# Grouped attention layers: values' last two quarters joined in the next tile, denominators joined with its first quarter, reciprocals on 16 columns

## What is computed

```
xn   = x * rsqrt(mean(x*x) + eps) * w
q    = xn @ wq                    # 16 heads of 32
k, v = context @ wk, context @ wv # 4 heads of 32, each shared by 4 heads of q
out  = softmax(q k^T / sqrt(32)) v
x    = x + out @ wo
```

## Time and profile before

| | |
|---|---|
| median of 3 runs | 4080.01 us (4079.27 to 4080.47) |
| the profiled execution | 4083.46 us |
| its span, first to last instruction | 4081.7 us |
| granted TensorE clock, mean | 0.989 of full |
| TensorE busy | 3991.6 us, 98% |
| VectorE, ScalarE, GpSimd busy | 2434.2, 2094.2, 2035.3 us |

### The profile page before, as it was taken

How to read it: one execution, slowest core, us unless ns; L and a number is a source line. 1 busy time by engine, 2 the same in 40 slices (tenths; PEclk the granted TensorE clock), 3 DMA queues, 4 the chain that set the end, 5 groups by cost and what they waited for, 6 DMA issues and landing times. The chain is left out here.

```text
span 4081.7 us, 52317 instructions
## 1 busy us (share of the span) xinstructions
PE 3991.6 (98%) x19446; PEld 2636.9 (65%) x19446; DVE 2434.2 (60%) x3455; ACT 2094.2 (51%) x2728; POOL 2035.3 (50%) x1097
## 2 busy tenths in 40 slices
PE   9999999998999999999968999999999999999999
PEld 7888888886566666666544555555555555555555
DVE  3221210011755566556638888888888888888885
ACT  3111221121544454444527776776677677767765
POOL 0000000001655566556736777677667677776766
PEclk9999999998999999999979999999999999999999
DMA  5343522233645555555423333333333333333332
GB/s 185 129 135 133 170 96 85 79 114 91 161 125 139 136 135 134 137 135 132 116 70 88 88 89 88 100 101 100 84 100 91 90 99 98 99 89 92 100 78 67
DMA packets 312792, 447.01 MB, mean 110 GB/s; under 512 B 44728, under 2 KB 116408, under 8 KB 312552
## 3 DMA queue, kind: packets, MB, share of 16 engines
q1 hardware_dynamic: 312552, 443.84, 38.8%
HBM read 215.07 MB, written 102.77 MB: 78 GB/s over the span
## 5 line engine op out<-in xcount | busy, mean ns | idle before, releaser
L1943 DVE TENSOR_REDUCE a_max_cols<-a_ps 128x1 f32<-128x512 f32 x1536 | 1028.5, 675 | 265.5 <-PE a_ps L2077 257.2
L1826 ACT ACTIVATE a_probs<-a_ps 128x1024 f32<-128x1024 f32 x768 | 774.6, 1024 | 378.3 <-PE a_ps L2108 372.7
L2077 PE MATMUL a_ps<-a_k_ops,a_q_ops 96*128 96x512 f32 x1536 | 653.3, 427 | 24.1 <-DVE a_max_cols L1943 17.5
L1724 POOL TENSOR_TENSOR a_sums<-a_probs 128x1024 f32<-128x1024 f32 x192 | 455.3, 2391 | 336.0 <-ACT a_probs L1826 336.0
L1047 DVE TENSOR_REDUCE a_max_cols<-a_ps 128x1 f32<-128x512 f32 x512 | 340.8, 688 | 273.4 <-PE a_ps L1211 273.3
L2077 PEld LDWEIGHTS a_ps<-a_k_ops,a_q_ops 96*128 96x128 f32 x1536 | 291.8, 190 | 312.5 <-issue 141.6
L2108 PE MATMUL a_ps<-a_q_ops,a_k_ops 128*128 128x512 f32 x1536 | 486.6, 398 | 1.1 <-ACT a_probs L1826 1.1
L807 POOL MEMSET a_ident<- 128x128 f32 x1 | 0.2, 204 | 975.5 <-issue 975.5
L1724 POOL TENSOR_TENSOR a_sums<-a_sums,a_probs 128x1024 f32<-128x1024 f32 x192 | 454.4, 2389 | 0.1
L2122 PE MATMUL a_ps<-a_probs,a_v 128*32 128x512 f32 x3072 | 411.1, 607 | 0.7 <-ACT a_probs L1826 0.6
L303 DVE TENSOR_TENSOR cp_c_lo<-cp_raw,cp_c_hi 128x1024 fp32r<-128x1024 f32 x64 | 78.4, 1226 | 529.2 <-ACT cp_c_hi L247 529.1
(11 more groups left out here) (154 smaller groups left out, 7347.0 us busy)
## 6 DMA issues: line engine op xcount, KB each, us to landing
a_k_ops<-k_scratch SPq DMA_DIRECT2D x192, 256.0 KB, 4.4
a_q_ops<-a_qn_hi SPq DMA_DIRECT2D x768, 64.0 KB, 2.0
k_scratch<-cp_out SPq DMA_DIRECT2D x88, 512.0 KB, 2.8
cp_raw<-in_ctx_t SPq DMA_DIRECT2D x64, 512.0 KB, 4.1
a_q_ops<-a_qn_hi SPq DMA_DIRECT2D x256, 128.0 KB, 2.3
x_raw<-out_t SPq DMA_DIRECT2D x25, 1024.0 KB, 7.2
a_q_ops<-a_qn_lo SPq DMA_DIRECT2D x384, 64.0 KB, 2.0
a_x_res<-out_t SPq DMA_DIRECT2D x92, 256.0 KB, 3.1
```

The costliest lines, as they stand in the source:

```text
L1724: pool.tensor_tensor(sums[:, hp], (probs if n < H else sums)[:, hp], probs[:, n], ALU.add)\
L1826: act.activation(probs[:, n], ps[:, 2 * (n % 2):2 * (n % 2) + 2, :], ACT.Exp).then_inc(exped, 1)
L1943: dve.tensor_reduce(max_cols[:, t % 2, col:col + 1], bank(b), AX.X, ALU.max, negate=True)\
L2077: pe.matmul(bank(b), q_ops[0:SHIFT, s, h, q * P:(q + 1) * P], k_ops[0:SHIFT, s, :], start=True, stop=True).then_inc(smax, 1)
```

## The change

Quarters 2 and 3 of a tile's values both run in the next tile, after its maximum 0. The denominators run there too, but after quarter 0 of that next tile. The denominators no longer pass ScalarE: VectorE transposes them by blocks of 32 x 32 out of PSUM (`turn_denominators`), which leaves each head's 512 values in 16 columns; it inverts these (`reciprocal`), spreads them again by a second transpose (`spread_reciprocals`), and does the product itself (`normalise`). The mean square goes the same way (`turn_squares`, `invert_mean_square`, `spread_roots`). GpSimd's first two sums of a tile wait for the denominators of the tile before, and its third addition of squares moves from the end of tile 1 into tile 2.

```diff
-    def sum_squares(n):
-        for k in range(1, CK):
+    def sum_squares(n, quarters=range(1, CK)):
+        for k in quarters:
             pool.wait_ge(sq_step, n * SQ + k)
             pool.tensor_tensor(sq[:, 0, :], sq[:, 0, :], sq[:, k, :], ALU.add).then_inc(sq_step, 1)
...
@@ -1718,7 +1723,9 @@
     def sum_probs(it, t, n):
         g, hp = tile_no(it, t), n % (H // 2)
-        if n >= H:
+        if n < H:
+            wait(pool, den_done, g)
+        else:
             pool.wait_ge(summed, g * SUMS + n - H + 1)
         pool.wait_ge(exped, g * NS + n + 1)
         pool.tensor_tensor(sums[:, hp], (probs if n < H else sums)[:, hp], probs[:, n], ALU.add)\
...
-        pool.tensor_tensor(stage[:, t % 2, :], out_raw[:, :], stage[:, t % 2, :], ALU.mult).then_inc(normed, 1)
...
@@ -1751,12 +1752,12 @@
             sum_probs(it, t, 3)
             if there(it, t + AHEAD):
                 rest_q(*at(it, t + AHEAD))
+            if t == 2 and there(it, 2 * T):
+                sum_squares(it + 2, range(CK - 1, CK))
             sum_probs(it, t, 4)
             sum_probs(it, t, 5)
-            if there(it, t - 1):
-                normalise(*at(it, t - 1))
             if t == 1 and there(it, 2 * T):
-                sum_squares(it + 2)
+                sum_squares(it + 2, range(1, CK - 1))
             if t == 2 and there(it, 2 * T):
                 rest_squares(it + 2)
...
     def inv_rms(n):
-        act.wait_ge(ms_step, MS * (n + 1))
-        act.activation(inv[:, :], ms[:, :], ACT.Sqrt, scale=scale * scale).then_inc(inv_done, 1)
+        act.wait_ge(ms_step, 2 * (n + 1))
+        act.activation(inv_col[:, :, :], ms_col[:, :, :], ACT.Sqrt, scale=scale * scale).then_inc(roots, 1)
...
-    def take_denominators(it, t):
-        g = tile_no(it, t)
-        act.wait_ge(den_done, g + 1)
-        wait(act, o_lo, g - 1)
-        act.activation(stage[:, t % 2, :], bank(FB), ACT.Copy).then_inc(den_taken, 1)
...
@@ -1848,14 +1842,12 @@
                 round_output(*at(it, t - 2), par if t >= 2 else 1 - par)
             if there(it, t - 1):
                 take_outputs(*at(it, t - 1))
-                take_denominators(*at(it, t - 1))
...
                 squares(1)
-            if t == 1 and there(it, T):
-                act.wait_ge(q_taken, (it + 1) * T)
+            if t == (1 if it == 0 else 0) and there(it, T):
                 inv_rms(it + 1)
             exponential(it, t, 2)
...
-    def mean_square(n, from_bank):
+    def turned_cols():
+        return cols[:, :, :].rearrange("p i j -> p (i j)")
+    def inverted(it, t):
+        return min(it + 2 + (t == T - 1), N)
+    def turn_squares(n, from_bank):
         dve.wait_ge(ssum_done, n + 1)
-        wait(dve, inv_done, n)
-        dve.tensor_scalar(ms[:, :], bank(from_bank), 1.0 / C, EPS, ALU.mult, ALU.add).then_inc(ms_step, 1)
-    def invert_mean_square(n, i):
-        w = S // PARTS
-        if i == 0:
-            dve.wait_ge(ms_step, MS * n + 1)
-        part = ms[:, i * w:(i + 1) * w]
-        dve.reciprocal(part, part).then_inc(ms_step, 1)
+        if n > 1:
+            dve.wait_ge(recip_made, (n - 2) * T + T - 2)
+        dve.transpose(turned_cols(), bank(from_bank)).then_inc(ms_turned, 1)
+    def invert_mean_square(n):
+        dve.wait_ge(ms_turned, n + 1)
+        wait(dve, roots, n)
+        dve.tensor_scalar(ms_col[:, :, :], cols[:, :, 0:1], 1.0 / C, EPS, ALU.mult, ALU.add).then_inc(ms_step, 1)
+        dve.wait_ge(ms_step, 2 * n + 1)
+        dve.reciprocal(ms_col[:, :, :], ms_col[:, :, :]).then_inc(ms_step, 1)
+    def spread_roots(n):
+        dve.wait_ge(roots, n + 1)
+        wait(dve, q_taken, n * T)
+        dve.transpose(inv[:, :].rearrange("p (i j) -> p i j", j=d), inv_col[:, :, :].broadcast_to([P, S // d, d]))\
+            .then_inc(inv_done, 1)
...
-    def reciprocal(it, t, i):
+    def turn_denominators(it, t):
         if there(it, t):
-            n = S // PARTS
-            if i == 0:
-                dve.wait_ge(den_taken, tile_no(it, t) + 1)
-            part = stage[:, t % 2, i * n:(i + 1) * n]
-            dve.reciprocal(part, part).then_inc(recip_done, 1)
+            g = tile_no(it, t)
+            dve.wait_ge(den_done, g + 1)
+            wait(dve, recip_made, g)
+            dve.wait_ge(ms_step, 2 * inverted(*at(it, t + 1)))
+            dve.transpose(turned_cols(), bank(FB)).then_inc(den_turned, 1)
+    def reciprocal(it, t):
+        if there(it, t):
+            g = tile_no(it, t)
+            dve.wait_ge(den_turned, g + 1)
+            wait(dve, recip_done, g)
+            dve.reciprocal(recip_col[:, :, :], cols[:, :, 0:1]).then_inc(recip_made, 1)
+    def spread_reciprocals(it, t):
+        if there(it, t):
+            g = tile_no(it, t)
+            dve.wait_ge(recip_made, g + 1)
+            wait(dve, o_lo, g - 1)
+            dve.transpose(stage[:, t % 2, :].rearrange("p (i j) -> p i j", j=d),
+                          recip_col[:, :, :].broadcast_to([P, S // d, d])).then_inc(recip_done, 1)
+    def normalise(it, t):
+        if there(it, t):
+            g = tile_no(it, t)
+            dve.wait_ge(recip_done, g + 1)
+            dve.wait_ge(out_taken, g + 1)
+            dve.tensor_tensor(stage[:, t % 2, :], out_raw[:, :], stage[:, t % 2, :], ALU.mult)\
+                .then_inc(normed, 1)
...
@@ -1975,64 +2004,65 @@
         for t in range(T):
             maximum(it, t, 0)
             if t == 0 and not first and there(it, T):
-                invert_mean_square(it + 1, 2)
-                invert_mean_square(it + 1, 3)
+                split_x(it + 1, 1)
             if t == 1 and there(it, T):
                 for k in range(0 if first else 2, CK):
                     split_x(it + 1, k)
             if t == 3 and there(it, 2 * T):
                 split_x(it + 2, 0)
-                split_x(it + 2, 1)
             maximum(it, t, 1)
             maximum(it, t, 2)
             if t == 1:
                 where(dve, it, par, 1, lambda: rest_wo(it // B))
-            reciprocal(*at(it, t - 1), 0)
             maximum(it, t, 3)
+            if t == T - 1 and there(it, 2 * T):
+                turn_squares(it + 2, OUTB)
             maximum(it, t, 4)
-            reciprocal(*at(it, t - 1), 1)
+            if t == T - 1 and there(it, 2 * T):
+                invert_mean_square(it + 2)
+            if t == 1 and first:
+                spread_roots(1)
             maximum(it, t, 5)
             if there(it, t + AHEAD):
                 take_q(*at(it, t + AHEAD))
             maximum(it, t, 6)
             if t == 0 and first:
-                mean_square(1, FB)
-            if t == T - 1 and there(it, 2 * T):
-                mean_square(it + 2, FB)
+                turn_squares(1, FB)
+            turn_denominators(*at(it, t - 1))
             maximum(it, t, 7)
             maximum(it, t, 8)
-            reciprocal(*at(it, t - 1), 2)
+            if t == 0 and first:
+                invert_mean_square(1)
+            reciprocal(*at(it, t - 1))
             maximum(it, t, 9)
+            spread_reciprocals(*at(it, t - 1))
             maximum(it, t, 10)
             if there(it, t - LAG):
                 add_result(it, t)
             maximum(it, t, 11)
-            reciprocal(*at(it, t - 1), 3)
-            if t == 0 and first:
-                for i in range(PARTS):
-                    invert_mean_square(1, i)
+            normalise(*at(it, t - 1))
             maximum(it, t, 12)
-            if t == T - 1 and there(it, 2 * T):
-                invert_mean_square(it + 2, 0)
             maximum(it, t, 13)
+            if t == 0 and not first and there(it, T):
+                spread_roots(it + 1)
             maximum(it, t, 14)
-            if t == T - 1 and there(it, 2 * T):
-                invert_mean_square(it + 2, 1)
             if t == 0 and there(it, T):
                 where(dve, it, par, B - 1, lambda: rest_wq(it // B + 1))
             maximum(it, t, 15)
...
+    invert_mean_square(0)
     rest_wq(0)
+    spread_roots(0)
...
-    for i in range(PARTS):
-        reciprocal(N - 1, T - 1, i)
+    turn_denominators(N - 1, T - 1)
+    reciprocal(N - 1, T - 1)
+    spread_reciprocals(N - 1, T - 1)
+    normalise(N - 1, T - 1)
...
@@ -2056,7 +2086,7 @@
         if not there(it, t):
             return
         if 0 in tiles:
-            wait(pe, den_taken, tile_no(it, t) - AHEAD)
+            wait(pe, shifted, 2 * (tile_no(it, t) - AHEAD + 1))
...
         for k in tiles:
@@ -2094,7 +2124,8 @@
             pe.wait_ge(added, g - LAG)
         else:
             pe.wait_ge(q_taken, g + AHEAD)
-            pe.wait_ge(ms_step, 2 * MS if t > 0 else 2 * MS + 1)
+            pe.wait_ge(ms_turned, 2)
+            wait(pe, den_turned, g - 1)
...
@@ -2117,6 +2148,8 @@
             if t == 0:
                 pe.wait_ge(v_in, (it + 1) * DMA)
             wait(pe, out_taken, g)
+            if t == T - 1 and there(it, 2 * T):
+                pe.wait_ge(ms_turned, it + 3)
...
@@ -2132,6 +2165,8 @@
```

(23 more changed lines are left out.)

23 lines of the change are left out of this document (10 added, 13 removed).

## The result

The changed kernel takes 4395.24 us (median of 4 runs, 4392.49 to 4401.29) against 4080.12 us of the kernel before beside it: 1.0775 times, 95% interval 1.0756 to 1.0793. The forecast was 4266 us with a range of 4140 to 4290; the direction was right, the size was not.

What follows compares the result with a forecast made beforehand. TensorE, busy 98% of the span, was taken to set the time, with tile ends mattering most. 35 + 38 + 108 + 15 - 4 - 6 = +186 on 4083.5 gives 4270, less 3.45: 4266 us, range 4140 to 4290.

Steps and rivals of the forecast that it cites:

- The predicted +186: Sum of all priced terms over the whole kernel, in us, added to the profiled 4083.5.
- Joined quarters: End of each tile: next tile's first scores wait for exponential 6, +0.39 a tile, +35 us over 91 tiles.
- Blocked product: Product on VectorE waits for GpSimd's third sum: +1.62 in the 67 tiles of t = 0, 1 and 3, +108 us.
- The near-tie: Starts of GpSimd's sum and VectorE's product 0.04 apart; sum taken as first; rival, product first: 4162 us, chance 0.26.
- Tile 2: At t = 2 ScalarE's rounding of squares waits for GpSimd's third addition: +1.73 in 22 tiles, +38 us; tile about 22.
- Spreading the roots at t = 0: VectorE step between reductions of M13 and M14: 0.69 longer if blocked (+15 us in 22 tiles), 0.33 unblocked (+7).
- Tile 3: At t = 3 the projection's wait for the mean square goes, 0.18 net, -4 us.
- The VectorE transposes: Transposes replacing reciprocals, taken as 0.69 each like a reduction of 512 columns; no cost where the product is blocked.
- the 16-column reciprocal: Small reciprocal on VectorE, estimated 0.1 to 0.2 us with 0.5 of room.
- Edges: Start of the grouped work: four reciprocals (3.39) shrink to some 0.5 and the turn's 3.41 wait goes, -6 us.
- the last rival: New TensorE idle stretches lower the granted clock: over 4300 us; part of the 0.08 chance above 4290.

Runs made afterwards that it cites:

- fill: The changed kernel with six extra matmuls of zeros per tile between the last scores and maximum 14; 4271.49 us.
- n_pool_sq: The changed kernel with the product back on GpSimd behind its fourth sum and the third addition of squares back at the end of tile 1; 4144.41 us.
- n_pool: The changed kernel with only the product put back on GpSimd, behind its fourth sum; 4208.29 us.
- cols16: The kernel before with denominators and mean squares inverted on 16 columns, nothing else moved but the matmuls summing a batch's squares; 4067.74 us.
- wait_longer: The kernel before with an added VectorE reduction (mean 2.76 us) behind the reciprocal's fourth part, making TensorE wait; 4445.71 us.
- wait_long: The kernel before with an added VectorE reduction of about 2.0 us behind the reciprocal's fourth part, from the sixth tile on; 4253.85 us.
- fill2: The changed kernel with two extra matmuls of zeros per tile between scores 7 and maximum 14; 4301.12 us.

## Why the prediction was right and wrong

**The sum.** The predicted +186 was for the waits, and the run that has the changed kernel's waits but not its clock (fill) measured +189 over the 4082.11 beside it: 4271.49 where 4266 was forecast. Part by part:
- Joined quarters, +0.39 a tile, +35: measured 0.44 (n_pool_sq, 20.37 against 19.93), 40 us. Right, for the reason given: S0 waits for exponential 6.
- Blocked product, +1.62 in 67 tiles, +108: measured 1.45 (fill 21.82 against n_pool 20.37), 97 us. The near-tie was called for the blocked side, and it fell there in nearly every tile (a median of 2.89 us for a 0.69 us instruction). With two starts forecast 0.04 apart, that the call came out is partly luck.
- Tile 2, 22.05 forecast: 22.7 in fill. The mechanism is as described (3.10 us of wait on ScalarE, S0 behind it), its size 0.65 short in 22 tiles, 14 us. Why S0 comes that much later was not taken apart.
- Spreading the roots at t = 0, +0.69: measured 0.76 blocked (fill, 22.58 against 21.82) and 0.42 unblocked (forecast 0.33).
- Tile 3, -4 us: not there in the changed kernel's order (0.66 over its neighbours in n_pool_sq, 0.65 before), but there in cols16 (0.46).
- The VectorE transposes, taken as 0.69: 0.72 out of PSUM, 0.70 for the spread; the 16-column reciprocal 0.23, where 0.1 to 0.2 was estimated. Hidden, as said.
- Edges, -6: cols16 puts edges and tile 3 together at -15, so this was undersized.

The parts are off in both directions, by +5, -11 and +14 us among others, so the total of fill is closer than its parts deserve.

**The step that failed** is the last rival: "New stretches of idle TensorE lower the granted clock: over 4300. No row of this trace bears it out for gaps this short." It was given part of a chance of 0.08, and it is what happened; the rows it says are missing were in the trace (below). The step behind it is that I priced 2 us of new idle time per tile as 2 us per tile. It cost 2 and then 1.4 to 1.6 more, since the work behind it ran at half clock, and it was the joined quarters that stood there. Of the 129 us by which the forecast was short, 124 are this, shown by filling the wait (84 half-clock stretches to 4, 4395 to 4271 us) and, in the kernel before, by making it (wait_longer).

**What the trace of before could have told.** The earlier trace rows has a matmul that waited 3.41 us, and the prediction read only the wait. The stretch right behind it, of the same trace:

```profile
2144.00:2148.00 4.00, 0.59 (x9) 0.14 (x2) 3.74 (x5) 1.23 (x2) 3.11 (x2) 0.77 0.42 98
2148.00:2151.50 3.50, 3.50 (x11) 2.75 (x11) 1.38 (x2) 2.19 (x3) 0.00 (x0) 0.50 0.40 94
```

The granted clock is 0.50 right behind a wait of 3.4 us, though it had been down just ahead of the wait as well (0.66 from 2140 to 2144). Nearer still are the waits that the earlier trace rows counts, whose longest is 2.6. Three of the ten are that long, at 2239.79, 2886.19 and 3534.23. Behind the first the clock stayed at 1.00; behind the second and the third TensorE ran at half clock:

```profile
2886.19 0.50 PE L2077 MATMUL a_ps<-a_k_ops,a_q_ops 96*128 96x512 f32 x1 [2.60 <-DVE a_max_cols L1943]
2888.98 1.66 PE L2122 MATMUL a_ps<-a_probs,a_v 128*32 128x512 f32 x8
```

```profile
2887.00:2890.00 3.00, 3.00 (x13) 1.23 (x12) 2.41 (x4) 1.73 (x3) 2.53 (x2) 0.50 0.13 38
```

These two are the only half-clock stretches inside the stage between its first 30 us and its end. That isn't proof for 2 us, but these are rows for the rival, and with 91 such places in the sum it deserved a price of its own: by my estimate, made with the 1.5 us that the later runs show, 91 times 1.5 is 137 us, which added to 4266 gives 4403.

The Trainium skill (TensorE: Matmul & The Clock Gate, "HAM oscillation — how this bites in real kernels") describes a kernel that falls back to half clock behind the wait of each of its iterations. The trace agrees with the pattern: such a fall in 79 of 89 tiles. It does not agree with the length of gap that the section names, which is longer than any wait of these tiles; by that rule alone the clock would have held and the time been near 4271 us. The measurement decides. The prediction did not weigh this section.

**Open.** Which property of the idle time decides (its length, its share of some stretch, what precedes it) isn't settled; the runs show outcomes for 1.5 and for 2.0 to 2.3 us in this one place of this one kernel. Length alone doesn't decide it, since tiles with the same waits came out both ways in wait_long, wait_longer, fill2 and the changed kernel. No run moved the waits in time while keeping their length.

## What to carry to other kernels

Where the sum gives TensorE new idle time that repeats, look at the granted clock behind the waits the trace already has, price the work behind the new ones at half clock as well, and look which work that is; a few matmuls of zeros in a wait that can't be avoided can be worth more than they cost (two of 0.23 us won back 1 us a tile here). An instruction on VectorE with two inputs in SBUF can take as long as what GpSimd is running or has queued at that moment (0.69 became 2.91 between two sums in a row, and 3.98 behind three instructions), so it belongs where GpSimd is idle, or on GpSimd itself; a lead of 0.1 us is no design. Join stretches where nobody waits for what follows them, and take an operation that fills a catch-up pause for what it is: moving it saves nothing.
